# Attention rows solved without a scaled copy of the probabilities, with the small products' operands exchanged and the next expert tile turned earlier

## The reference, cut to what matters

```python
probs = jax.nn.softmax(logits + causal_mask, axis=-1)          # 8 batches x 16 heads, 512 positions
L = jnp.eye(s) - jnp.tril(probs, -1)
rhs = jnp.diagonal(probs, axis1=-2, axis2=-1)[..., None] * v
A = jax.scipy.linalg.solve_triangular(L, rhs, lower=True)      # row t needs all rows before t
...
h = gelu(einsum('ecd,edf->ecf', exp_batches, c_fc)); exp_out = einsum('ecf,efd->ecd', h, c_proj)
```

## Time and profile before

| | us |
|---|---|
| median of 3 runs (1408.22 to 1410.42) | 1409.95 |
| the profiled execution, its own time | 1409.06 |
| span of its records | 1407.1 |
| VectorE / TensorE / ScalarE / GpSimd busy in the span | 910.4 / 979.8 / 466.4 / 342.9 |
| rows of one sub-block (first product to last reduction), 16 of them | 17.6 |
| between the rows of two sub-blocks of a block, 12 of them, in sum | 148.6 |
| from the start of a solve_block to its first row, four of them | 6.2 |

### The profile page before, as it was taken

How to read it: one execution, slowest core, us unless ns; L and a number is a source line. 1 busy time by engine, 2 the same in 40 slices (tenths; PEclk the granted TensorE clock), 3 DMA queues, 4 the chain that set the end, 5 groups by cost and what they waited for, 6 DMA issues and landing times. The chain is left out here.

```text
span 1407.1 us, 29569 instructions
## 1 busy us (share of the span) xinstructions
PE 979.8 (70%) x10741; PEld 766.5 (54%) x10762; DVE 910.4 (65%) x3559; ACT 466.4 (33%) x1066; POOL 342.9 (24%) x390
## 2 busy tenths in 40 slices
PE   5376599970665057876769967769986768986754
PEld 5265499960621034665646556646665656765643
DVE  5666272216789065788858889858878970068767
ACT  1233244424224003311235411235522227931115
POOL 1277155540047170021210021210001220012221
PEclk9998799995579587966889966889977888986777
DMA  9397598836018864410044220044411005420008
GB/s 225 40 212 206 145 250 241 230 96 179 25 50 238 244 149 123 111 28 18 25 97 129 73 61 20 21 110 126 116 44 32 26 22 163 137 57 23 25 22 234
DMA packets 241824, 153.95 MB, mean 109 GB/s; under 512 B 80432, under 2 KB 226096, under 8 KB 241424
## 3 DMA queue, kind: packets, MB, share of 16 engines
q1 hardware_dynamic: 232528, 133.04, 37.1%
q0 software_dynamic: 9152, 19.02, 4.1%
HBM read 96.76 MB, written 55.24 MB: 108 GB/s over the span
## 5 line engine op out<-in xcount | busy, mean ns | idle before, releaser
L1157 DVE TENSOR_REDUCE mx<-banks 128x1 f32<-128x384 f32 (+3 forms) x352 | 203.1, 635 | 74.0 <-PE banks L1088 58.9
L1323 DVE TENSOR_TENSOR prod<-A,Kst_Pn 128x8 f32<-128x8 f32 (+30 forms) x992 | 179.5, 221 | 0.5
L1329 DVE TENSOR_REDUCE A<-prod 128x4 f32<-128x8 f32 (+30 forms) x992 | 174.8, 217 | 0.0
L800 POOL DMA_INDIRECT o_dram<-step_o,step_to x80 | 81.9, 1024 | 308.5 <-ACT step_o L789 296.3
L1137 ACT ACTIVATE Eoff<-banks 128x256 f32<-128x256 f32 (+2 forms) x192 | 114.9, 599 | 102.6 <-PE banks L1073 93.5
L1071 PE MATMUL banks<-Qexp,Kst_Pn 128*128 128x256 bf16 x640 | 115.4, 282 | 47.5 <-DMA Qmax<-q_stack 37.8
L1139 ACT ACTIVATE Ed<-banks 128x256 f32<-128x256 f32 x256 | 97.9, 382 | 111.5 <-PE banks L1073 111.5
L1084 PE MATMUL banks<-masks,identb 128*128 128x128 bf16 (+2 forms) x352 | 89.2, 254 | 61.0 <-DMA Qmax<-q_stack 51.1
L756 PE MATMUL banks<-step_xT,step_w 128*128 128x256 f32 x320 | 106.3, 490 | 22.5 <-issue 22.0
L1263 POOL TENSOR_TENSOR A<-A,Kst_Pn 128x256 f32<-128x256 f32 x16 | 15.8, 987 | 411.6 <-DVE Kst_Pn L1293 411.6
L1088 PE MATMUL banks<-Kst_Pn,Qmax 128*128 128x128 bf16 (+3 forms) x491 | 115.7, 306 | 0.0
(11 more groups left out here) (197 smaller groups left out, 1832.5 us busy)
## 6 DMA issues: line engine op xcount, KB each, us to landing
Kst_Pn<-k_stack SPq DMA_DIRECT2D x32, 512.0 KB, 4.1
rows_dram<-blank SPq DMA_DIRECT2D x12, 858.0 KB, 11.6
e_w<-in_L_w1T_dram SPq DMA_DIRECT2D x39, 256.0 KB
e_w<-in_L_w2T_dram SPq DMA_DIRECT2D x39, 256.0 KB
Qmax<-q_stack SPq DMA_DIRECT2D x64, 96.0 KB
Qexp<-q_stack SPq DMA_DIRECT2D x64, 96.0 KB
Kst_Pn<-k_stack SPq DMA_DIRECT2D x16, 384.0 KB, 4.3
step_xt<-rows_dram SPq DMA_DIRECT2D x40, 132.0 KB, 2.2
```

The costliest lines, as they stand in the source:

```text
L800: self.nc.gpsimd.indirect_dma_start(self.o_dram, bass.IndirectOffsetOnAxis(self.to[n][:, j:j + 1], 0), self.o[n][:, j, :], None).then_inc( ...
L1157: nc.vector.tensor_reduce(out, logits, AX_X, ALU.max, negate=True).then_inc(max_done, 1)
L1323: nc.vector.tensor_tensor(prod[:, ds, 0:r + 1], A[:, ds, k0:k0 + r + 1], Pn[:, c * SUB + r:c * SUB + r + 1, 0:r + 1].broadcast_to([P, HD / ...
L1329: nc.vector.tensor_reduce(A[:, ds, k0 + r], prod[:, ds, 0:r + 1], AX_X, ALU.add).then_inc(row_done, 1)
```

## The change

Five things change, all in `solve_block` (the tile `later_term` is gone, `later` is a quarter as large):

1. ScalarE copies the turned exponentials as they are into `Pn` (`keep_probs`), one sub-block ahead, in place of VectorE's multiplication by `rZ`. GpSimd's diagonal work (`own`) also runs one sub-block ahead.
2. `before` and `later` are added to `A` unscaled (`add_sums`). Row 0 of a sub-block is multiplied by its `rZ`, and each row product becomes a `scalar_tensor_tensor`, which multiplies `A` by the row's own `rZ` (one value per partition, read from a tile) and by `Pn`.
3. `turn_before(c+1)` stands behind `keep_rows(c-1)` and in front of `add_later(c)`; the reciprocal stays at the head of `add_before(c)`.
4. In `later_sums` the operands are exchanged: `Ed` is stationary, 8 columns of `Apos` move.
5. The turn of tile k+1 stands between `up(k)` and `down(k)`, across sub-blocks too.

```diff
@@ solve_block, tensor
-                        last = nc.tensor.matmul(wide[SUB * g:SUB * (g + 1), t * SUB:(t + 1) * SUB], Apos[0:c * SUB, row:row + SUB],
-                                                Ed[0:c * SUB, SUB * g + t, c * SUB:(c + 1) * SUB], start=True, stop=True,
-                                                skip_group_check=True)
+                        last = nc.tensor.matmul(wide[SUB * g:SUB * (g + 1), t * HD:(t + 1) * HD],
+                                                Ed[0:c * SUB, SUB * g + t, c * SUB:(c + 1) * SUB], Apos[0:c * SUB, row:row + HD],
+                                                start=True, stop=True, skip_group_check=True)
...
                 for k in tiles[c]:
-                    steps.turn(pe, k)
+                    if k == tiles[0].start:
+                        steps.turn(pe, k)
                     steps.up(pe, k)
+                    if k + 1 < tiles[-1].stop:
+                        steps.turn(pe, k + 1)
                     steps.down(pe, k)
@@ solve_block, scalar
+            def keep_probs(c):
+                for g in range(per_sub * c, per_sub * (c + 1)):
+                    if g:
+                        act.wait_ge(probs_turned, g)
+                    nc.scalar.copy(Pn[:, g * TURN:(g + 1) * TURN, :],
+                                   bank[g % 2][:, 0:TURN * SUB].rearrange("p (q k) -> p q k", k=SUB)).then_inc(probs_in, 1)
+
+            keep_probs(0)
             for c in range(NSUB):
+                if c + 1 < NSUB:
+                    keep_probs(c + 1)
@@ solve_block, vector
             def turn_before(c):
                 base(nc.vector.transpose(before[:, :, :], RT[:, c, :, :].rearrange("p t q -> p q t")))
+
+            def add_before(c):
                 base(nc.vector.reciprocal(rZ[:, c * SUB:(c + 1) * SUB], before[:, :, HD]))
...
+                dve.wait_ge(own_done, 2 * c + 2)
+                add_sums(c, before[:, :, 0:HD].rearrange("p q d -> p d q"))
...
-                base(nc.vector.transpose(later[:, :, :], wide[:, :].rearrange("p (t q) -> p q t", q=SUB)))
-                add_term(c, later)
+                base(nc.vector.transpose(later[:, :, :], wide[:, 0:SUB * HD].rearrange("p (t d) -> p d t", d=HD)))
+                add_sums(c, later[:, :, :])
...
-                        nc.vector.tensor_tensor(prod[:, ds, 0:r + 1], A[:, ds, k0:k0 + r + 1],
-                                                Pn[:, c * SUB + r:c * SUB + r + 1, 0:r + 1].broadcast_to([P, HD // 2, r + 1]),
-                                                ALU.mult).then_inc(row_done, 1)
+                        nc.vector.scalar_tensor_tensor(out=prod[:, ds, 0:r + 1], in0=A[:, ds, k0:k0 + r + 1], scalar=rZ[:, q0 + r:q0 + r + 1],
+                                                       in1=Pn[:, q0 + r:q0 + r + 1, 0:r + 1].broadcast_to([P, HD // 2, r + 1]),
+                                                       op0=ALU.mult, op1=ALU.mult).then_inc(row_done, 1)
```

More of the change, by code:

```diff
@@ L947, in solve_attention @@
         prod = sb("prod", [P, HD, SUB])
-        later, term = sb("later", [P, SUB, SUB]), sb("later_term", [P, SUB, HD])
+        later = sb("later", [P, HD, SUB])
         mx = sb("mx", [P, 2, BH])
@@ L978, in solve_attention @@
             if I >= 0:
-                solve_block(nc, I, Ed, RT, before, rZ, Pn, prod, later, term, A, Apos, ident, bank, big[3], steps)
+                solve_block(nc, I, Ed, RT, before, rZ, Pn, prod, later, A, Apos, ident, bank, big[3], steps)
 def attend(nc, I, A, vT_dram, ident, Kst, Qmax, Qexp, k_stack, q_stack, max_dram, mx, mxp, mxT, masks,
@@ L1180, in turn_probs, with solve_block @@
     return last
-def solve_block(nc, I, Ed, RT, before, rZ, Pn, prod, later, term, A, Apos, ident, bank, wide, steps):
+def solve_block(nc, I, Ed, RT, before, rZ, Pn, prod, later, A, Apos, ident, bank, wide, steps):
     k0 = I * steps.N // LT
@@ L1215, in turn_rows @@
             def turn_rows(c):
-                pe.wait_ge(row_done, ops * (c + 1))
+                pe.wait_ge(row_done, (ops + 1) * (c + 1))
                 for d in range(HD):
@@ L1246, in _ @@
         def _(act):
+            def keep_probs(c):
[5 more added lines that the diff above has]
+            keep_probs(0)
             for c in range(NSUB):
+                if c + 1 < NSUB:
+                    keep_probs(c + 1)
                 for k in tiles[c]:
-                    steps.keep_turned(act, k)
+                    if k == tiles[0].start:
+                        steps.keep_turned(act, k)
                     steps.gelu(act, k)
+                    if k + 1 < tiles[-1].stop:
+                        steps.keep_turned(act, k + 1)
                     steps.keep_out(act, k)
@@ L1257, in _, with own @@
         def _(pool):
-            for c in range(NSUB):
+            def own(c):
                 ts = slice(t0 + c * SUB, t0 + (c + 1) * SUB)
@@ L1266, in _ @@
                 nc.gpsimd.memset(diag, 1.0).then_inc(own_done, 1)
+            own(0)
+            for c in range(NSUB):
+                if c + 1 < NSUB:
+                    own(c + 1)
                 for k in tiles[c]:
@@ L1274, in _, with add_sums @@
             base = Chain(dve, base_done)
[L1276 to L1277 removed]
+            def add_sums(c, sums):
                 ts = slice(t0 + c * SUB, t0 + (c + 1) * SUB)
[L1279 to L1282, removed]
+                base(nc.vector.tensor_tensor(A[:, :, ts], A[:, :, ts], sums, ALU.add))
             def turn_before(c):
                 base(nc.vector.transpose(before[:, :, :], RT[:, c, :, :].rearrange("p t q -> p q t")))
+            def add_before(c):
                 base(nc.vector.reciprocal(rZ[:, c * SUB:(c + 1) * SUB], before[:, :, HD]))
[L1288 to L1296 removed]
+                dve.wait_ge(own_done, 2 * c + 2)
+                add_sums(c, before[:, :, 0:HD].rearrange("p q d -> p d q"))
             def keep_rows(c):
@@ L1329, in _ @@
                         nc.vector.tensor_reduce(A[:, ds, k0 + r], prod[:, ds, 0:r + 1], AX_X, ALU.add).then_inc(row_done, 1)
+                    n += 4
             keep_rows(NSUB - 1)
```

22 lines of the change are left out of this document (8 added, 14 removed).

## The result

The changed kernel takes 1439.97 us (median of 4 runs, 1437.36 to 1443.73) beside 1410.18 before (4 runs, 1408.22 to 1412.49): the ratio is 1.0206, 95% interval 1.0182 to 1.023. It is slower, as forecast, but by 29.8 us where 6.5 were predicted, and outside the range of 1397 to 1430. The profiled execution took 1439.94, its span 1438.0; against the profiled execution of before that is 30.9 more, and the four solve blocks, from their first instruction to SyncE's first DMA of the next stage, account for 30.2 of it (481.5 before, 511.7 after, sums over the blocks).

What follows compares the result with a forecast made beforehand. VectorE bounds the rows; in gaps it waits for GpSimd, then TensorE's small products, whose instructions arrive in pieces of 256. Rows +61.3, gaps -39.6, starts -2.8, ends -12.4: +6.5 on 1409.06 gives 1415.6 us, range 1397 to 1430.

Steps and rivals of the forecast that it cites:

- The rows: Row products of the 16 sub-blocks: a scalar read from a tile costs 0.062 to 0.064 per product, +61.3 us in all.
- The bound named there: GpSimd's diagonal beside the rows, in 12 places: at most its own 1.06 us each, at least nothing; nothing was taken.
- The gaps: The 12 stretches between rows of two sub-blocks: 3.6 us each plus 65.8 of small products, 109.0 against 148.6, so -39.6.
- from the last reduction to the copy of the turned rows 1.15: First piece of each gap after the change: 1.15 us until VectorE's copy, reciprocal and first add lying under that wait.
- the small products: TensorE's 128 products in each gap: 67.4 us before, 65.8 after in sum, with bounds of 69.5 and 31.
- The nine gains of 0.4: Small products in nine of twelve gaps: 0.4 us saved each, only on what stands behind the last instruction stop.
- The third rival: TensorE becomes the bound: idle longer, its tiles run at 1.2 GHz and end late; 10.4 us more, 1426; chance 0.13.
- Block starts: From a solve block's start to its first rows: 5.5 us in place of 6.20, four times -0.7, so -2.8.
- Block ends: Last reduction to next stage: VectorE's drain sets the end instead of GpSimd's, -3.1 us four times, -12.4, at least -4.
- The exchange and the stops: Small products: 8 columns moving save little, since instructions arrive in pieces of 256; the third block's first gap gains a stop, +2.0.
- the second rival: Instructions arrive in time: the small products take 2.6 us each, 31 in place of 65.8, total 1381; chance 0.06.
- the first rival: Scalar read hidden in the rows: +19 in place of 61.3, TensorE a little late in sub-block 2, +3: 1377; chance 0.11.

Runs made afterwards that it cites:

- with TensorE at work: The changed kernel plus extra TensorE products of constants behind the last 10, 7, 3 and 7 rows of a block's four sub-blocks: 1421.52 us.
- 48 more: The changed kernel plus 12 small products of constants (48 instructions) on TensorE, once, at the start of the first solve block: 1432.71 us.

## Why the prediction was wrong, point by point

- **The rows: +61.3 forecast, +62.7 measured, right by two errors.** The scalar cost 55 (0.056 per product; 0.062 to 0.064 was taken from the earlier trace rows). That is below the 0.058 at which the prediction's own sum changes its sign: with 55 in place of 61.3 it gives about nothing. So that the direction came out as forecast is luck too; the steps below that failed made it. GpSimd's diagonal was costed at nothing, because its sends beside the rows showed no idle time; but sends are not products, and its product held up one row in each of twelve sub-blocks by 0.6. The bound named there, 1.06 each, held.
- **The gaps: -39.6 forecast, -26.7 measured; this is the largest failed step.** The piece "from the last reduction to the copy of the turned rows 1.15" was taken from a place where TensorE came straight from its tiles. The same section worked out that the tiles would end earlier and the rows later, and so made TensorE idle there, but did not carry the clock into the turn, though the kernel before had two turns of 1.74 and 1.91 behind some 2 us without work. The piece measured 2.0 on average: 10 of the 12.9 that are missing. The other 2.9 are the small products (65.8 forecast, 68.7 measured). The third block's first gap got its second stop as foreseen (5.6 to 7.0). The nine gains of 0.4 behind the last stop came to 0.5 at most in all: a product takes TensorE 30 ns by its own row (1.93 for 128 records, two to a product), not 26, and with 8 columns it takes as long (1.89). And in the first block the two stops moved from the second gap (7.8 to 5.0) to the third (4.8 to 8.0), which the prediction did not look at; why a first stop shows at one place and not at another stays open.
- **The third rival had the right cause in the wrong place.** It let the low clock lengthen the tiles until TensorE became the bound. TensorE is not late in any sub-block; the clock cost up to 0.9 in a turn of eight instructions that stands in the path whatever TensorE has to spare.
- **Block starts: -2.8 forecast, +4.2 measured.** The transposition of sub-block 1 was listed as moved behind the copy of the gap; at sub-block 0 there is no copy and no gap, and its 1.92 went into the path four times. The term was left out of the sum.
- **Block ends: -12.4 forecast, -10.0 measured.** That VectorE's drain takes over from GpSimd's was right; the slow turn took 0.9 back at each end, as the ends of 3.0 (3.5 in the last block) with TensorE at work show.
- **The exchange and the stops: right.** No gain in the small products from the exchange, stops 256 instructions apart at fixed places, the gain only in what VectorE does behind them. In no run do the 256 records of products take less than 4.5, where the second rival wanted 2.6. (A slip without weight: the terms of the first rival give 1376, not 1377.)

The misses add up: 1.4 + 12.9 + 7.0 + 2.4 = 23.7, of 24.4 between the two profiled sums (30.9 - 6.5).

## What to carry to other kernels

When a change moves an engine's work earlier, ask at which clock that engine does the next thing on the path: idle time won off the path can come back as a slow instruction on it. When an instruction is moved ahead in a loop, write out the first and the last turn of the loop by themselves, since there is no work there to hide it. A scalar read from a tile is a price per instruction, so apply it once to the operand that many small instructions read, not in each of them.

## What the runs showed of the hardware

- The scalar read from a tile costs 0.056 per product in a row of alternating products and reductions, and a number in the instruction nothing (17.65 for the last sub-block of a block, against 17.71 for plain products in the same place).
- A product of GpSimd of 0.85 to 0.91 holds up one product of VectorE beside it, by 0.6.
- TensorE's turn of the rows: 1.9 at granted clock 0.50 (1.2 GHz), seen behind 2.3 to 10.3 us without work; 1.03 to 1.10 at 1.00 (2.4 GHz), seen right behind other work and in some places behind up to 3.8 us without it.
- 512 load and product records take 4.6 to 5.7 with one stop inside and 7 to 8 with two, with 8 or 32 columns and at either clock. The Trainium skill says in Runtime: NRT & Kernel Launch, section Instruction fetch mechanics, that the fetching is mostly hidden behind the block before. If the stops of 1.1 to 2.7 are that fetching, it is not hidden here: their distance of 256 instructions and their move with 48 more speak for it, but no row names it.
